# Residual tiles and output laid out by row block, then sequence, then channel; residual loads in eight transfers a tile

## The chip, the core and the metric

The kernel runs on one core of a Trainium2 chip. A core has a matrix engine (TensorE, PE in the profile), a vector engine (VectorE, DVE), an activation engine (ScalarE, ACT), a general engine (GpSimd, POOL), and a sequencer that mostly issues DMAs (SyncE, SP); sixteen DMA engines move data between HBM and the on-chip memory SBUF. The metric is device time in microseconds of one execution, the median of several.

## What is computed

x is [32 sequences, 64 channels, 1024 positions] in float32. Four layers follow one another, each added to its input:

```python
x = x + L0(x)   # long convolution per channel (state-space kernel), masked by length
x = x + L1(x)   # einsum('bsi,boi->bso', x, weight[adapter])   1024 x 1024, one of 16 per sequence
x = x + L2(x)   # the same with a second set of weights
x = x + L3(x)   # gate and up (1024 -> 2752), silu(gate) * up, down (2752 -> 1024), each with a rank-16 adapter
```

The last line is where the change lies. Its `x +` needs the input of the last layer again, the residual, once the down projection has produced its part.

## The kernel before

Positions lie on the 128 partitions: position = 128 * l + partition, with l = 0..7 (LT = 8) the row block. A tile is TB = 8 sequences of H = 64 channels, 512 columns; there are NTILE = 4 tiles, handled in NST = 2 stages of two tiles each (j = 0, 1). The last layer's matmuls are split by a Strassen-like scheme with seven products, and every product in three passes of rounded high and low parts (`three`, lines 2289 to 2291).

After the second layer the input of the third is stored in HBM as `kept_rows` (`xs`, [P, B, LT, H]: for each partition sequence, then block, then channel). The down projection of a stage (`down(st)` on TensorE) runs through eleven products: d1, d5, l11, d2, d6, l21, d4, d7, l12, d3, l22. A d product has five panels, an l product two; together NSIDE = 43 panels, counted by `panel_done`. For each panel n, ScalarE rounds the weights and the activations to `wdh` and `th` and VectorE forms the low parts `wdl` and `tl` (helper line 1642), while SyncE loads the raw panels three ahead at most. The buffers of the cut panels are doubled.

Between these cuts, in an order written out by hand (`take_product(st, n)`), VectorE adds each finished product from the matmul banks, or from a carry (`tmp`), into the residual tiles `resid[0]` and `resid[1]` (helper line 1645). These additions are called takes here. A product in the banks has the shape [P, 4 blocks, 512 columns], columns being sequence times channel, while `resid` is [P, TB, LT, H] (sequence, block, channel): the take reads the banks with strides. Tile 0 is first needed at panel n = 9, tile 1 at n = 11, just between the cut of the side and the cut of the row that the first panel of d2 (n = 12) needs.

GpSimd issues the residual loads (`load_residual`, line 789): tile 0 once four panels have ended, tile 1 after seven. In stage 0 it then issues sixteen loads of the next stage's rows (`load_rows`, line 797, to `rraw`), four each after panels 9, 11, 13 and 16; these already read `kept_rows` one block at a time. Afterwards it stores the halves of the residual tiles as they become complete (`store`, line 783), and SyncE stores the last half tile in three parts (line 713). The waits on `resid_in` count 16 for each transfer. GpSimd does all this in order.

Of the kernel before, what the change touches and what calls it, by code (L numbers as in the profile page):

```python
# [16 lines left out]
F32 = mybir.dt.float32  # L17
# [5 lines left out]
P = 128  # L23
B, H, L = 32, 64, 1024
LT = L // P
# [29 lines left out]
NTILE = ROWS // TILE  # L55
TB = TILE // H
# [69 lines left out]
def sides(st, n):  # L126
    return st * NSIDE + n
# [31 lines left out]
def build(nc, ins, out):  # L159
    with ExitStack() as ctx:  # L160
        sem = lambda name: ctx.enter_context(nc.semaphore(name))

        def sb(stack, name, shape, dt=F32):
            return stack.enter_context(nc.sbuf_tensor(name, shape, dt))
# [3 lines left out]
        xs = nc.dram_tensor("kept_rows", [P, B, LT, H], F32).ap()  # L168
# [82 lines left out]
        def placed(offset, above="main"):  # L251

            s = ExitStack()
            if offset:
                sb(s, f"below_{above}", [P, offset // 4])
            return s
# [9 lines left out]
        with placed(OPS_AT) as s:  # L266
# [5 lines left out]
            rows = [sb(s, f"rows{k}", [P, KH, TILE], F32R) for k in range(14)]  # L272
# [1 line left out]
            tmp = sb(s, "tmp", [P, 6, TILE])  # L274
            lraw = sb(s, "lraw", [P, GR, 2, P])
        with placed(0) as s:
            resid = [sb(s, f"resid{j}", [P, TB, LT, H]) for j in range(2)]
        with placed(OPS_AT, "wdh") as s:
            wdh = sb(s, "wdh", [P, 2, LT * P], F32R)
            th0 = sb(s, "th0", [P, 2 * TILE], F32R)  # L280
# [18 lines left out]
        carry = tmp[:, 2:6]  # L299
# [21 lines left out]
        ps = ctx.enter_context(nc.psum_tensor("ps", [P, 8, 512], F32))  # L321
# [94 lines left out]
        taken = sem("taken")  # L416
        carried = sem("carried")
        resid_in = [sem(f"resid_in{j}") for j in range(2)]
        y_out = sem("y_out")
        last_out = sem("last_out")  # L420
# [9 lines left out]
        def _(sp):  # L430
# [279 lines left out]
            for k, (ready, o, width) in enumerate(((10, 0, 4), (12, 4, 2), (14, 6, 2))):  # L710
                mine = slice(o, o + width)
                sp.wait_ge(taken, end + ready)
                sp.dma_start(out[NTILE - 1, :, :, mine], resid[1][:, :, mine]).then_inc(last_out, 16)
            sp.wait_ge(last_out, 48)

# [1 line left out]
        def _(pool):  # L718
# [22 lines left out]
            for k in range(2):  # L741
                pool.iota(spare[:, k].rearrange("l (t u) -> l t u", u=2), pattern=[[0, STEPS // 2], [k, 2]],
                          base=B + 2 * (1 - k), channel_multiplier=0,
# [39 lines left out]
            def store(st, ready, j, half):  # L783

                pool.wait_ge(taken, st * NTAKE + ready)
                mine = slice(4 * half, 4 * half + 4)
                pool.dma_start(out[2 * st + j, :, :, mine], resid[j][:, :, mine]).then_inc(y_out, 16)

            def load_residual(tile):

                pool.wait_ge(x_saved[tile // 2], 16)
                for part in range(4):
                    mine = slice(2 * part, 2 * part + 2)
                    b0 = tile * TB + 2 * part
                    pool.dma_start(resid[tile % 2][:, mine], xs[:, b0:b0 + 2]).then_inc(resid_in[tile % 2], 16)

            def load_rows(st, part):

# [6 lines left out]
            def down_loads(st):  # L805

                for ended, tile, part in ((4, 0, None), (7, 1, None), (9, None, 0), (11, None, 1), (13, None, 2), (16, None, 3)):
                    if part is not None and st:
                        continue
                    pool.wait_ge(panel_done, sides(st, ended))  # L810
                    if part is None:
                        load_residual(2 * st + tile)
                    else:
                        load_rows(st + 1, part)
# [32 lines left out]
            for s in range(SEQ):  # L847
                gather_inner(1, s)
                gather_outer(1, s)
            down_loads(0)  # L850
            store(0, 5, 0, 0)
            store(0, 8, 0, 1)
            store(0, 10, 1, 0)
            store(0, 14, 1, 1)
            pool.wait_ge(y_out, 64)
# [442 lines left out]
        def _(dve):  # L1298
# [315 lines left out]
            base = 0  # L1614
            for layer in range(2):
# [11 lines left out]
                base = base + count  # L1627
# [16 lines left out]
            def add(to, a, b):  # L1644
                return V.tensor_tensor(out=to, in0=a, in1=b, op=ALU.add)  # L1645
# [311 lines left out]
            def take(st, p, half, j, blocks=range(4)):  # L1957

                o0, n = blocks[0], len(blocks)
                base = BANKS[p] + o0  # L1960
                rows = resid[j][:, :, 4 * half + o0:4 * half + o0 + n]
                add(rows, ps[:, base:base + n].rearrange("p o (b h) -> p b o h", h=H), rows).then_inc(taken, 1)

            def add_carry(st, p, ready):

                dve.wait_ge(carried, 3 * st + ready)
                add(carry, ps[:, BANKS[p]:BANKS[p] + 4], carry).then_inc(carried, 1)

            def take_carry(st, ready, half, j):

                dve.wait_ge(carried, 3 * st + ready)
                rows = resid[j][:, :, 4 * half:4 * half + 4]
                add(rows, carry.rearrange("p o (b h) -> p b o h", h=H), rows).then_inc(taken, 1)

            def take_product(st, n):

                if n == 9:
                    dve.wait_ge(resid_in[0], (st + 1) * 64)
                    take_carry(st, 1, 0, 0)
                if n in (11, 12):  # L1980
                    dve.wait_ge(resid_in[1], (st + 1) * 64)
                    dve.wait_ge(panel_done, sides(st, SIDE_AT["l11"]))
                    take(st, "d5", 0, 1, range(2 * (n - 11), 2 * (n - 10)))
                if n == 13:
                    take(st, "d5", 1, 1)
                if n == 21:
                    dve.wait_ge(panel_done, sides(st, SIDE_AT["d6"]))
                    dve.wait_ge(taken, st * NTAKE + 1)
                    take(st, "d2", 0, 0)
                if n == 25:  # L1990
                    dve.wait_ge(panel_done, sides(st, SIDE_AT["l21"]))
                    add_carry(st, "d6", 1)
                if n == 33:
                    dve.wait_ge(panel_done, sides(st, SIDE_AT["d7"]))
                    take(st, "d4", 1, 0)
                if n == 34:
                    dve.wait_ge(taken, st * NTAKE + 3)
                    take_carry(st, 2, 0, 1)
                if n == 37:
                    dve.wait_ge(panel_done, sides(st, SIDE_AT["l12"]))  # L2000
                    dve.wait_ge(taken, st * NTAKE + 7)
                    add_carry(st, "d7", 2)
                if n == 38:
                    dve.wait_ge(taken, st * NTAKE + 6)
                    take_carry(st, 3, 1, 0)
                if n == 39:
                    dve.wait_ge(taken, st * NTAKE + 4)
                    take_carry(st, 3, 1, 1)
                if n == NSIDE - 1:
                    dve.wait_ge(panel_done, sides(st, SIDE_AT["l22"]))  # L2010
                    dve.wait_ge(taken, st * NTAKE + 7)
                    take(st, "d3", 0, 1)
# [105 lines left out]
            for st in range(NST):  # L2118
# [21 lines left out]
                for n in range(2, NSIDE):  # L2140
                    whole = n < NSIDE - 1 and n + 1 not in AFTER_SHORT
                    if whole:
                        add_side(st, n + 1)
                    panel_lo(st, n)
                    if whole:
                        add_row(st, n + 1)
                    if n + 2 in AFTER_SHORT:
                        add_side(st, n + 2)
                        add_row(st, n + 2)
                    if n == 3:  # L2150
                        down_ranks(st)
                    take_product(st, n)
                    if st == 0:
                        new_rows_lo(n)
# [440 lines left out]
```

## Time and profile before

| | |
|---|---|
| Median of 3 runs | 2087.67 us (2087.14 to 2090.92) |
| The profiled execution | 2089.7 us |
| Its span, first to last instruction | 2088.0 us |
| Granted TensorE clock, mean | 0.998 of full speed |
| TensorE matmul busy | 2025.6 us, 97% |
| VectorE busy | 1756.0 us, 84% |
| ScalarE busy | 989.9 us, 47% |
| GpSimd busy | 134.8 us, 6% |

All times in rows are microseconds from the start of the span, unless a row says ns. PE is TensorE's matmuls, PEld its weight loads. `L1642` is line 1642 of the kernel. A group of instructions is named by what it writes and reads (out<-in). "busy" is the time in which the engine executes. A wait is put down to what ended it; "issue" means that nothing the profile shows ended it.

### The profile page before, as it was taken

Reading aid. Unit: us, or ns where it says so; the run is one execution under the profiler, and the core shown is the slowest. Engines: PE = TensorE matmul, PEld = TensorE weight load, DVE = VectorE, ACT = ScalarE, POOL = GpSimd, SP = SyncE. Lnnn points to the kernel's source line nnn. Section 1 sums busy time; section 2 is a strip of 40 time slices with the busy share of each in tenths; the row PEclk is TensorE's granted clock in tenths of the full one; section 3 lists DMA queues with packets and bytes.
Section 4 is the critical chain, followed back from the end, with each engine's and each line's share of the span. In section 5 each row is a group of like instructions: output and inputs, shape, how many; then the busy total and the mean of one; then the engine's idle time right before and its main releaser. Section 6 shows DMA issues by size and latency. Waiting matters only on the chain.

```text
span 2088.0 us, 33689 instructions
## 1 busy us (share of the span) xinstructions
PE 2025.6 (97%) x10192; PEld 1722.8 (83%) x10192; DVE 1756.0 (84%) x2203; ACT 989.9 (47%) x1255; POOL 134.8 (6%) x229
## 2 busy tenths in 40 slices
PE   2999999999999999999999999999999999999998
PEld 1998888878888788888888888888888888888887
DVE  8796999999999988878787779979788787868787
ACT  2221888878886534343343443454343333434332
POOL 3100000000000323210000020010000000000000
PEclk9999999999999999999999999999999999999999
DMA  6997999999999556754334996645334333368665
GB/s 247 336 335 281 340 358 350 355 346 352 347 363 351 165 164 194 201 145 106 97 100 107 343 316 213 203 144 132 91 101 113 94 103 102 100 220 305 197 204 183
DMA packets 246432, 459.51 MB, mean 220 GB/s; under 512 B 110502, under 2 KB 113766, under 8 KB 226662
## 3 DMA queue, kind: packets, MB, share of 16 engines
q1 hardware_dynamic: 229250, 416.03, 59.6%
q0 software_dynamic: 14944, 42.50, 6.7%
q8 instruction: 30, 0.49, 0.1%
q10 hardware_dynamic: 2180, 0.26, 0.1%
q14 instruction: 28, 0.23, 0.0%
HBM read 418.56 MB, written 63.73 MB: 231 GB/s over the span
## 4 chain that ended last, share of the span: by engine, by line
PE 83%; DVE 9%; DMA 3%; issue 2%; ACT 2%; DVEq 0%; ACTq 0%; SPq 0%
PE ps L2289 19%; PE ps L2290 19%; PE ps L2291 19%; PE ps L2183 5%; PE ps L2211 5%; PE ps L2213 5%; PE ps L2212 5%; DMA W<-in_w 2%; PE ps L2367 2%; PE ps L2368 2%; DVE part L1550 1%; PE ps L2220 1%; PE ps L2404 1%; PE ps L2405 1%; DVE rows L1642 1%
## 5 line engine op out<-in xcount | busy, mean ns | idle before, releaser
L2289 PE MATMUL ps<-rows,oph 128*128 128x512 f32 x1196 | 467.2, 391 | 1.1 <-DVE opl L1642 0.6
L2290 PE MATMUL ps<-rows,oph 128*128 128x512 f32 x1196 | 466.9, 390 | 0.0
L2291 PE MATMUL ps<-rows,opl 128*128 128x512 f32 x1196 | 465.3, 389 | 0.0
L1550 DVE TENSOR_TENSOR part<-W,part 128x2048 fp32r<-128x2048 f32 x152 | 344.1, 2289 | 14.0 <-ACT part L902 13.2
L1645 DVE TENSOR_TENSOR tmp<-ps,tmp 128x512 f32<-128x512 f32 (+2 forms) x344 | 242.9, 707 | 106.0 <-PE ps L2368 61.0
L902 ACT ACTIVATE part<-W 128x2048 fp32r<-128x2048 f32 x152 | 290.9, 1917 | 84.5 <-DMA W<-in_w 58.5
L2291 PEld LDWEIGHTS ps<-rows,opl 128*128 128x128 f32 x1196 | 224.6, 188 | 47.7
L2289 PEld LDWEIGHTS ps<-rows,oph 128*128 128x128 f32 x1196 | 225.0, 188 | 45.5 <-DVE opl L1642 1.9
L2290 PEld LDWEIGHTS ps<-rows,oph 128*128 128x128 f32 x1196 | 225.0, 188 | 41.8
L2289 PE MATMUL ps<-th,wdh 128*128 128x512 f32 (+1 forms) x656 | 249.4, 380 | 1.6 <-DVE tl L1642 1.1
L2290 PE MATMUL ps<-tl,wdh 128*128 128x512 f32 (+1 forms) x656 | 248.6, 379 | 0.0
L2291 PE MATMUL ps<-th,wdl 128*128 128x512 f32 (+1 forms) x656 | 248.5, 379 | 0.0
L967 ACT ACTIVATE oph<-sraw 128x512 fp32r<-128x512 f32 x168 | 105.9, 631 | 284.9 <-PE ps L2291 255.6
L2211 PE MATMUL ps<-part,rh 128*128 128x512 f32 x600 | 237.3, 395 | 0.5 <-issue 0.3
L2213 PE MATMUL ps<-part,rl 128*128 128x512 f32 x600 | 233.8, 390 | 0.0
L2212 PE MATMUL ps<-part,rh 128*128 128x512 f32 x600 | 233.7, 389 | 0.0
L2183 PE MATMUL ps<-urev,toep 128*128 128x256 f32 (+7 forms) x1024 | 151.5, 311 | 9.2 <-issue 9.1
L2183 PEld LDWEIGHTS ps<-urev,toep 128*128 128x128 f32 x1024 | 147.0, 194 | 13.5 <-issue 9.6
L967 ACT ACTIVATE wdh<-wraw 128x1024 fp32r<-128x1024 f32 (+1 forms) x66 | 66.6, 1009 | 172.1 <-PE ps L2291 167.1
L2289 PEld LDWEIGHTS ps<-th,wdh 128*128 128x128 f32 x656 | 123.4, 188 | 27.4 <-issue 2.5
L2291 PEld LDWEIGHTS ps<-th,wdl 128*128 128x128 f32 x656 | 123.4, 188 | 23.3
L2290 PEld LDWEIGHTS ps<-tl,wdh 128*128 128x128 f32 x656 | 123.4, 188 | 22.7
(246 smaller groups left out, 3027.1 us busy)
## 6 DMA issues: line engine op xcount, KB each, us to landing
W<-in_w SPq DMA_DIRECT2D x152, 1024.0 KB, 7.1
raw<-in_wgu SPq DMA_DIRECT2D x168, 256.0 KB, 2.8
traw<-kept_acts SPq DMA_DIRECT2D x78, 512.0 KB, 4.9
wraw<-in_wd SPq DMA_DIRECT2D x70, 512.0 KB
toep<-kpad SPq DMA_DIRECT2D x32, 1024.0 KB, 8.8
lraw<-picked_b SPq DMA_DIRECT2D x88, 256.0 KB, 4.0
kept_acts<-tmp SPq DMA_DIRECT2D x84, 256.0 KB, 2.4
urev<-in_urev SPq DMA_DIRECT2D x32, 256.0 KB, 6.7
```

The source lines that it names most:

```text
L902: nc.scalar.activation(wh[c][:], W[:, c], ACT.Copy).then_inc(w_hi, 1)
L967: return nc.scalar.activation(to, src, ACT.Copy)
L1550: V.tensor_tensor(out=wl[c][:], in0=W[:, c], in1=wh[c][:].bitcast(F32), op=ALU.subtract).then_inc(w_lo, 1)
L1645: return V.tensor_tensor(out=to, in0=a, in1=b, op=ALU.add)
L2183: last = mm(ps[:, i % RING, (e + 1) * LT * B - n:(e + 1) * LT * B], lhsT=toep[:, i % RING, e, d * P:(d + 1) * P], rhs=rows[:, 0:n], start= ...
L2211: mm(bank(o), lhsT=rh[:, at], rhs=wh[c][:, k], start=first, stop=False)
L2212: mm(bank(o), lhsT=rh[:, at], rhs=wl[c][:, k], start=False, stop=False)
L2213: last = mm(bank(o), lhsT=rl[:, at], rhs=wh[c][:, k], start=False, stop=end)
L2289: mm(to, lhsT=wh, rhs=mh, start=start, stop=False)
L2290: mm(to, lhsT=wh, rhs=ml, start=False, stop=False)
L2291: return mm(to, lhsT=wl, rhs=mh, start=False, stop=stop)
L2367: mm(ps[:, to, cols], lhsT=lt[:, g, c], rhs=tmh[:, c, g], start=start and g % 2 == 0, stop=False)
```

## The change

`resid` and the output `y` get the order block, sequence, channel. A take then reads and writes one run of columns for each block, as the banks have them. The residual load is cut into eight transfers, one for each block, since `kept_rows` keeps its order (sequence, block, channel): a transfer reads, for each partition, eight pieces of 64 floats. The semaphore values follow, and the host puts the output in order with another transpose.

```diff
@@ -274,7 +274,7 @@
         with placed(0) as s:
-            resid = [sb(s, f"resid{j}", [P, TB, LT, H]) for j in range(2)]
+            resid = [sb(s, f"resid{j}", [P, LT, TB, H]) for j in range(2)]
@@ -710,7 +710,7 @@
                 mine = slice(o, o + width)
                 sp.wait_ge(taken, end + ready)
-                sp.dma_start(out[NTILE - 1, :, :, mine], resid[1][:, :, mine]).then_inc(last_out, 16)
+                sp.dma_start(out[NTILE - 1, :, mine], resid[1][:, mine]).then_inc(last_out, 16)
@@ -784,15 +784,14 @@
                 mine = slice(4 * half, 4 * half + 4)
-                pool.dma_start(out[2 * st + j, :, :, mine], resid[j][:, :, mine]).then_inc(y_out, 16)
+                pool.dma_start(out[2 * st + j, :, mine], resid[j][:, mine]).then_inc(y_out, 16)
 
             def load_residual(tile):
 
                 pool.wait_ge(x_saved[tile // 2], 16)
-                for part in range(4):
-                    mine = slice(2 * part, 2 * part + 2)
-                    b0 = tile * TB + 2 * part
-                    pool.dma_start(resid[tile % 2][:, mine], xs[:, b0:b0 + 2]).then_inc(resid_in[tile % 2], 16)
+                for l in range(LT):
+                    pool.dma_start(resid[tile % 2][:, l], xs[:, tile * TB:(tile + 1) * TB, l]
+                                   ).then_inc(resid_in[tile % 2], 16)
@@ -1958,8 +1957,8 @@
-                rows = resid[j][:, :, 4 * half + o0:4 * half + o0 + n]
-                add(rows, ps[:, base:base + n].rearrange("p o (b h) -> p b o h", h=H), rows).then_inc(taken, 1)
+                rows = resid[j][:, 4 * half + o0:4 * half + o0 + n].rearrange("p o b h -> p o (b h)")
+                add(rows, ps[:, base:base + n], rows).then_inc(taken, 1)
@@ -1969,16 +1968,16 @@
-                rows = resid[j][:, :, 4 * half:4 * half + 4]
-                add(rows, carry.rearrange("p o (b h) -> p b o h", h=H), rows).then_inc(taken, 1)
+                rows = resid[j][:, 4 * half:4 * half + 4].rearrange("p o b h -> p o (b h)")
+                add(rows, carry, rows).then_inc(taken, 1)
 
             def take_product(st, n):
 
                 if n == 9:
-                    dve.wait_ge(resid_in[0], (st + 1) * 64)
+                    dve.wait_ge(resid_in[0], (st + 1) * LT * 16)
                     take_carry(st, 1, 0, 0)
                 if n in (11, 12):
-                    dve.wait_ge(resid_in[1], (st + 1) * 64)
+                    dve.wait_ge(resid_in[1], (st + 1) * LT * 16)
@@ -2587,8 +2586,8 @@
-    out = nc.dram_tensor("y", [NTILE, P, TB, LT, H], F32, kind="ExternalOutput").ap()
+    out = nc.dram_tensor("y", [NTILE, P, LT, TB, H], F32, kind="ExternalOutput").ap()
-    return np.ascontiguousarray(y.transpose(0, 2, 4, 3, 1).reshape(B, H, L))
+    return np.ascontiguousarray(y.transpose(0, 3, 4, 2, 1).reshape(B, H, L))
```

## Rows read from the trace of the kernel before

**Rows 1.** The page's busy line, and TensorE's waits in 1150 to 1400 us.

```profile
PE 2025.6 (97%) x10192; PEld 1722.8 (83%) x10192; DVE 1756.0 (84%) x2203; ACT 989.9 (47%) x1255; POOL 134.8 (6%) x229
...
PE ps L2289 <- DVE tl L1642: 1.1, 2, 0.7
```

**Rows 2.** VectorE by form, 1150 to 1400 us: busy us, mean ns, idle before.

```profile
L1645 DVE TENSOR_TENSOR resid<-tmp,resid 128x2048 f32<-128x2048 f32 x4 | 9.1, 2286 | 0.0
L1645 DVE TENSOR_TENSOR resid<-ps,resid 128x2048 f32<-128x2048 f32 x4 | 9.1, 2285 | 0.0
...
L1645 DVE TENSOR_TENSOR tmp<-ps,tmp 128x2048 f32<-128x2048 f32 x2 | 4.6, 2287 | 0.0
```

**Rows 3.** GpSimd's timeline, stage 0: start, duration, engine, line, count, [idle before].

```profile
1179.50 2.13 POOL L795 DMA_DIRECT2D resid<-kept_rows  x4 [271.45 <-PE ps L2291]
1196.65 2.08 POOL L795 DMA_DIRECT2D resid<-kept_rows  x4 [15.02 <-issue]
1206.70 3.55 POOL L802 DMA_DIRECT2D rraw<-kept_rows  x4 [7.97 <-PE ps L2291]
1215.01 2.64 POOL L802 DMA_DIRECT2D rraw<-kept_rows  x3 [4.77 <-PE ps L2291]
1225.75 4.37 POOL L802 DMA_DIRECT2D rraw<-kept_rows  x5 [8.11 <-issue]
```

**Rows 4.** Instructions on `kept_rows`: ns min/median/max, first and last start.

```profile
L795 POOL DMA_DIRECT2D resid<-kept_rows x16: 527/536/564, 1179.5 to 1907.9; - x16
L802 POOL DMA_DIRECT2D rraw<-kept_rows x16: 882/882/915, 1206.7 to 1242.2; - x16
```

**Rows 5.** Single `rraw` loads in short windows: their start and their landing.

```profile
L802 POOL DMA_DIRECT2D rraw<-kept_rows x1: 915/915/915, 1206.7 to 1206.7; - x1
DMA to landing us min/median/max: 4.7/4.7/4.7
...
L802 POOL DMA_DIRECT2D rraw<-kept_rows x1: 884/884/884, 1216.8 to 1216.8; - x1
DMA to landing us min/median/max: 8.5/8.5/8.5
...
L802 POOL DMA_DIRECT2D rraw<-kept_rows x2: 882/882/882, 1228.4 to 1229.2; - x2
DMA to landing us min/median/max: 8.8/9.8/10.7
```

**Rows 6.** GpSimd's DMA queue, packets, MB, share; 1178 to 1196, 1206 to 1250.

```profile
q0 software_dynamic: 576, 2.10, 32.1%
...
q0 software_dynamic: 1280, 4.20, 38.1%
```

**Rows 7.** Timeline of VectorE and TensorE around the first takes, stage 0.

```profile
1204.42 2.29 DVE L1645 TENSOR_TENSOR resid<-tmp,resid 128x2048 f32<-128x2048 f32 x1
...
1213.32 1.23 DVE L1645 TENSOR_TENSOR resid<-ps,resid 128x1024 f32<-128x1024 f32 x1
...
1215.90 1.23 DVE L1642 TENSOR_TENSOR wdl<-wraw,wdh 128x1024 fp32r<-128x1024 f32 x1 [0.23 <-ACT wdh L967]
...
1217.30 0.39 PE L2289 MATMUL ps<-th,wdh 128*128 128x512 f32 x1
```

**Rows 8.** The same in stage 1: tile 1 loaded and first used.

```profile
1906.33 2.10 POOL L795 DMA_DIRECT2D resid<-kept_rows  x4 [14.15 <-PE ps L2291]
...
1923.83 1.23 DVE L1645 TENSOR_TENSOR resid<-ps,resid 128x1024 f32<-128x1024 f32 x1
```

**Rows 9.** VectorE's timeline: the reader of the first eight `rraw` loads.

```profile
1232.69 2.29 DVE L1642 TENSOR_TENSOR rraw<-rraw 128x2048 f32<-128x2048 f32 x1 [0.78 <-DMA rraw<-kept_rows]
```

**Rows 10.** The end: SyncE's stores and wait; its DMA queue, 2079 to 2088 us.

```profile
2079.13 3.47 SPq L713 DMA_DIRECT2D y<-resid  x3
...
SPq L160 <- DMA y<-resid: 5.0, 1, 5.0
...
q1 hardware_dynamic: 3120, 2.10, 76.4%
```

## Prediction

> **What bounds the kernel now.** I read the page's busy shares first: the matmul engine is busy 97% of the span [rows 1]. So a saving on any other engine is worth nothing unless the matmul engine waits for it, and a new delay counts as soon as the work queued for it runs out. The change touches only the two down-projection stages (roughly 1180 to 1375 us and 1890 to 2088 us). The list of waits for the first of them shows the matmul engine waiting for VectorE twice, 1.1 us in all [rows 1]. The stages are therefore bound by TensorE, with VectorE close behind. In them VectorE cuts the operands of each panel of weights and does the "takes" (adding a product to a residual tile) between the cuts. The questions are: do the takes get shorter, do the residual tiles still come in time, and what does the end cost?
>
> **Takes.** All 28 change from blocks of 64 floats with strides to one run. In the trace a take of 128x2048 with the old strides is 2286 or 2285 ns, and the same size without any stride (`tmp<-ps,tmp`, the carry) is 2287 ns [rows 2]. Strides of this kind cost nothing here, so the takes stay as they are: 0 us, bounds within 0.1.
>
> **Residual loads, issue.** Before, a tile is four transfers of 0.53 us on GpSimd (4 KB in one piece per partition). After, it is eight, each made of 1024 pieces of 256 B. That is exactly the form of the 16 loads of `rraw` from `kept_rows` in line 802, which take 0.88 us each to issue [rows 4]. A tile's issue grows from 2.1 to 7.0 us.
>
> **Residual loads, transfer.** Four loads of a tile used 32.1% of 16 engines in 18 us, or 92 engine-us for 2.10 MB: 44 per MB. The 16 `rraw` loads used 38.1% in 44 us, or 268 for 4.20 MB: 64 per MB [rows 6]. A tile becomes 134 engine-us, 2.6 us more of all 16 engines. The Trainium skill, "DMA: Bandwidth & Descriptors", section on why small descriptors are slow, gives 11 cycles where 8 move data for a 256 B descriptor; as an estimate that makes 127 engine-us instead of 134. The rows show somewhat more than the page, and I go by the rows.
>
> **Residual loads, a wait in the queue.** In the timeline of GpSimd, loads of this form start at 1206.70 (four) and 1215.01 (three); the eighth, which waits for no semaphore of the program, starts only at 1225.75, after 8.11 us that the trace puts down to "issue" [rows 3]. The seventh was issued 1.76 us after 1215.01 and landed 8.5 us later, at 1225.27 [rows 5]: 0.48 us before the eighth started. I read this as room for seven such transfers in the queue of descriptors, and a wait for the seventh to land (they share a semaphore) before the eighth is written. The Trainium skill, same page, section "SWDGE vs HWDGE vs iDMA", says that GpSimd appends these descriptors to rings in a reserved part of SBUF. It states no such wait; only the row shows one. A tile after the change is eight such transfers in a row on one semaphore, so I expect the eighth of every tile to wait likewise: four waits, two in each stage.
>
> **When does a tile land?** From its first issue: the first load lands after 4.7 us [rows 5] to 6.9 us (issued at 1225.75, its reader starts at 1232.69) [rows 3, 9]. The next ones follow at the pace of the engines. Lower bound 134/8/16 = 1.05 us each, if nothing else moves; upper bound 1.8 us, the pace of five in a row beside SyncE's panel loads (the first lands by 1232.69, the fifth at 1229.2 + 10.7 = 1239.9, four steps) [rows 5, 9]. I take 1.6, nearer to the upper one, since SyncE's loads are in flight here too. The seventh lands at 4.7 + 6 x 1.6 = 14.3 us (bounds 11.0 and 17.7); the eighth is issued 0.5 later and lands in 5.5 us (4.7 to 6.9). The tile is there after 20.3 us (16.2 to 25.1), where now it takes some 10 us.
>
> **Tile 0** starts at 1179.50 and is first used at 1204.42 [rows 3, 7], 24.9 us later: covered, but for the upper bound by 0.2 us. **Tile 1** starts at 1196.65 and is used at 1213.32 [rows 3, 7], 16.7 us later. It lands at 1216.95, 3.6 us late. Behind that take VectorE has queued the row cut and the cut `wdl` at 1215.90 (which waited 0.23 for ScalarE and ends at 1217.13), and TensorE starts on that panel at 1217.30 [rows 7]. The slack is 0.23 + 0.17 = 0.4 us, so TensorE loses 3.2 us (bounds 0 and 8.0). In the second stage tile 1 starts at 1906.33 and is used at 1923.83 [rows 8], 17.5 us: 2.8 us late, 2.4 lost with the same slack (0 to 7.2). TensorE has no idle time later in which to make this good.
>
> **What stands behind tile 1 on GpSimd.** The `rraw` loads due at 1206.70 [rows 3] start at about 1212.4. Their consumer on VectorE at 1232.69 already waits 0.78 us for them [rows 9], but it will itself be 3.2 us late by then. I take 0.3 us (0 to 3). The slower transfers also squeeze SyncE's panel loads; the cover is the 1.2 to 2 us by which VectorE's cuts lead TensorE. Nothing in the trace prices this beyond the 1.1 us of rows 1; I take 0.3 us (0 to 2).
>
> **Stores.** Their runs in HBM grow from 1 KB (512 B for the last two) to 8 KB (4 KB). Nobody waits for the six that GpSimd issues while TensorE works on; I cost them at nothing, and their cover is the matmuls of the following panels (a single one of them costs a few tenths of a us if it were bare). The last three are bare: SyncE issues them from 2079.13 on and then waits 5.0 us for them. They use 76.4% of 16 engines in 9 us for 2.10 MB, 52 engine-us per MB, in 3120 packets [rows 10]. At the 44 per MB of 4 KB packets [rows 6] that is 8 x 2.1 / 16 = 1.1 us less, and the last issue gets a little shorter: -1.2 us (-2 to 0).
>
> **Sum.** 3.2 + 2.4 + 0.3 + 0.3 - 1.2 = +5.0 us. The profiled execution took 2089.7 us, of which 2088.0 are the span and 1.7 lie around it; it would become 2094.7. The median of the runs is 2.0 us below the profiled one, so I predict 2087.7 + 5.0 = 2092.7 us.
>
> **Rivals.**
> The tile comes in time (not slower). If the eighth load doesn't wait, it lands at 4.7 + 7 x 1.6 = 15.9 us, before the 16.7 of tile 1. The 8.11 us would then be something particular to that moment; it is a single event, which speaks for this rival, and its end on the landing of the seventh speaks against it. The same comes out if it waits but the transfers keep near the 1.05 us pace. Then 0.5 us of side costs and -1.2 remain: 2087.0 us. The turning point is a tile in 17 us. Chance 0.35.
> Pile-up (clearly slower). The transfers run at 1.8 us or worse, tile 0's eighth load goes out after 1196.65 and pushes tile 1, and each stage loses near its upper bound: 7 + 6 + 1 - 1.2, about +13 us, 2100.5 us. Against it: SyncE's loads pause while VectorE stands still, which lets the others through. Chance 0.10.
> Cheaper takes (faster). If single runs made VectorE faster after all, the last take, which nothing covers, would shorten, and the late tile would be caught up partly. Against it stand the equal durations of rows 2. To be faster by over 4 us TensorE would have to have been waiting for VectorE, and rows 1 give 1.1 us. About 2084 us, chance 0.03.
> The stores don't change: if the packets at the end stay small, the sum only loses its -1.2: 2093.9 us, inside the forecast's own range.
>
> **How the numbers follow.** A measurement of this kernel tells about 0.2%, 4.2 us, from no change. The forecast, a late tile 1, has a chance of 0.52 and its own range is 2089.5 to 2098; a good quarter of it ends under 2091.9. So slower by over 0.2%: 0.38 + 0.10 = 0.48. Within 0.2%: 0.35 + 0.14, with the rounding 0.48. Faster: 0.04. The range reaches from just under the first rival to the top of the forecast, 2086.3 to 2098.0; it leaves out the pile-up, the cheaper takes and some of the edges.
>
> **What would show it.** In the timeline of GpSimd after the change: eight loads a tile of 0.88 us, seven and then a gap of 7 to 9 us, four times. In VectorE's waits: the first `resid<-ps` of 128x1024 in each stage waiting for `resid<-kept_rows`, some 3 us. In TensorE's waits: the same, less 0.4, at the first panel of `d2`. The takes at 2285 ns as before. Some 500 packets instead of 3072 in the last stores, and SyncE's last wait near 4 us. The prediction is wrong if the gap is missing, if the tile lands within 17 us of its start despite it, or if VectorE's cuts after the late take turn out to have more slack than 0.4 us.

## The result, and the profile after

The changed kernel took 2100.39 us (median of 4 runs, 2098.84 to 2103.28), the kernel before, on the same chip, 2087.40 us. The ratio is 1.0057 [1.0045, 1.0068]: slower by some 12 us by the ratio (13.0 us between the medians), above the forecast of 2092.7 us and above its range (2086.3 to 2098.0). It is the number that the rival "pile-up" gave, 2100.5 us, though not for its reasons alone, as shown further down. The profiled execution took 2099.75 us, and its span is 2098.1 us against 2088.0 us before: the rows have 10.1 us to explain; the rest is where the two profiled executions lie among their runs.

The page's busy line:

```profile
PE 2026.9 (97%) x10192; PEld 1724.0 (82%) x10192; DVE 1755.5 (84%) x2203; ACT 990.9 (47%) x1255; POOL 152.6 (7%) x245
```

Beside [rows 1] only GpSimd's line has moved, by 16 instructions and 18 us of issuing. VectorE does what it did. Nothing in the busy shares tells of 10 us, because the loss lies in a few waits of TensorE. These are its waits in 1150 to 1400 us (stage 0), then in 1870 to 2099 us (stage 1), each with total, number and longest in us:

```profile
PE ps L2288 <- DVE wdl L1641: 5.9, 1, 5.9
PE ps L2288 <- DVE tl L1641: 1.4, 2, 0.7
...
PE ps L2288 <- DVE tl L1641: 2.2, 1, 2.2
PE ps L2288 <- DVE wdl L1641: 1.8, 1, 1.8
```

Before there were 1.1 us in stage 0 [rows 1] and none of this kind in stage 1. To see who is late, go back one step: the timeline of VectorE (lines 1641 and 1644), of ScalarE (966) and of TensorE (2288) around these waits, first stage 0, then stage 1 (start, duration, what, and in brackets the idle time and what ended it):

```profile
1219.16 1.23 DVE L1644 TENSOR_TENSOR resid<-ps,resid 128x1024 f32<-128x1024 f32 x1 [7.42 <-DMA resid<-kept_rows]
1222.71 0.80 PE L2288 MATMUL ps<-th,wdh 128*128 128x512 f32 x1 [5.89 <-DVE wdl L1641]
...
1929.66 1.06 ACT L966 ACTIVATE th<-traw 128x1024 fp32r<-128x1024 f32 x1 [3.98 <-DMA traw<-kept_acts]
1930.75 1.23 DVE L1641 TENSOR_TENSOR tl<-traw,th 128x1024 fp32r<-128x1024 f32 x1 [3.82 <-ACT th L966]
1932.12 0.36 PE L2288 MATMUL ps<-th,wdh 128*128 128x256 f32 x1 [2.17 <-DVE tl L1641]
1936.19 1.23 DVE L1644 TENSOR_TENSOR resid<-ps,resid 128x1024 f32<-128x1024 f32 x1 [3.61 <-DMA resid<-kept_rows]
1939.74 0.50 PE L2288 MATMUL ps<-th,wdh 128*128 128x512 f32 x1 [1.76 <-DVE wdl L1641]
```

In stage 0 the first take into tile 1 starts at 1219.16 us instead of 1213.32 us [rows 7], and the panel of d2 behind it at 1222.71 instead of 1217.30. In stage 1 two things are late: first `traw`, a panel of activations that SyncE loads, and then tile 1 again.

GpSimd's timeline shows why tile 1 is late (stage 0, then stage 1):

```profile
1178.78 6.19 POOL L793 DMA_DIRECT2D resid<-kept_rows  x7 [270.23 <-issue]
1193.76 7.01 POOL L793 DMA_DIRECT2D resid<-kept_rows  x8 [8.79 <-issue]
1212.28 0.88 POOL L793 DMA_DIRECT2D resid<-kept_rows  x1 [11.51 <-issue]
...
1897.62 6.17 POOL L793 DMA_DIRECT2D resid<-kept_rows  x7 [505.24 <-PE ps L2290]
1913.28 6.13 POOL L793 DMA_DIRECT2D resid<-kept_rows  x7 [9.49 <-issue]
1919.89 0.88 POOL L793 DMA_DIRECT2D resid<-kept_rows  x1 [0.48 <-issue]
1930.97 0.88 POOL L793 DMA_DIRECT2D resid<-kept_rows  x1 [10.20 <-issue]
```

A tile is seven loads and then, after a gap, the eighth: the gaps are 8.79, 11.51, 9.49 and 10.20 us. The rows merge what follows without idle time: the one at 1193.76 with its eight loads is tile 0's eighth with the first seven of tile 1 right behind it, and the one at 1913.28 is tile 0's eighth with six of tile 1, whose seventh is the row at 1919.89 and whose eighth is the one at 1930.97. Before, GpSimd's queue had 15.02 us of rest between the tiles [rows 3]; now the tiles touch. The landings in stage 0 of tile 0's eighth load together with tile 1's first (5.7 us the former alone, so 6.0 us the latter), then of tile 1's seventh, then of its eighth:

```profile
L793 POOL DMA_DIRECT2D resid<-kept_rows x2: 882/883/884, 1193.8 to 1194.6; - x2
DMA to landing us min/median/max: 5.7/5.9/6.0
...
L793 POOL DMA_DIRECT2D resid<-kept_rows x1: 891/891/891, 1199.9 to 1199.9; - x1
DMA to landing us min/median/max: 12.0/12.0/12.0
...
L793 POOL DMA_DIRECT2D resid<-kept_rows x1: 882/882/882, 1212.3 to 1212.3; - x1
DMA to landing us min/median/max: 6.9/6.9/6.9
```

The seventh lands at 1211.9 us and the eighth goes out at 1212.28, as [rows 3, 5] had it with 0.48 us between the two. The tile is complete at 1219.16 us.

Then there is a loss that stands in no wait. The windows of 1222 to 1228 and 1236 to 1242 us: length, busy time of PE, PEld, DVE, ACT, POOL with counts, then the granted clock, the share of the DMA engines and GB/s:

```profile
1222.00:1228.00 6.00, 5.29 (x13) 4.14 (x13) 6.00 (x5) 0.00 (x0) 0.00 (x0) 0.50 1.03 250
1236.00:1242.00 6.00, 6.00 (x29) 4.95 (x28) 4.11 (x3) 2.01 (x2) 0.00 (x0) 1.00 1.01 310
```

After its 5.9 us of idling TensorE was granted 0.50 of its clock, that is 1.2 GHz, until about 1228.7 us. Thirteen matmuls of 512 columns followed each other at 0.43 us where they do at 0.23 us from 1236 us on: 2.7 us.

Last the end: SyncE's stores, its wait for them, and the packets of its queue in the last 9 us. They answer to [rows 10]:

```profile
2091.18 3.03 SPq L713 DMA_DIRECT2D y<-resid  x3
...
SPq L160 <- DMA y<-resid: 3.4, 1, 3.4
...
q1 hardware_dynamic: 432, 2.10, 56.8%
```

432 packets instead of 3120, 56.8% of the engines instead of 76.4%, and 0.4 + 1.6 = 2.0 us gained.

The account: stage 0 lost 5.9 + 0.3 us in waits and 2.7 at half the clock, stage 1 lost 2.2 + 1.8 us, the end gave back 2.0 us: 10.9 us. The kernel came to the first of the two stages 0.7 us earlier (1178.78 against 1179.50). That leaves 10.2 us, against 10.1 in the spans. So close a match is partly luck: GpSimd's first load of stage 1 goes out at 1897.62 instead of 1890.02 us, 7.6 us later, where the account up to there has 8.2, and stage 1 has half a us more than its waits.

### The profile page after: what moved, and what is told of

Read it like the earlier page. It is cut to its first block, busy times and chain, and to the rows that moved or that the text cites. A ratio compares the mean times of both kernels' runs of the same rounds, so it can differ in the third digit from the quotient of the medians.

```text
span 2098.1 us, 33705 instructions
## 1 busy us (share of the span) xinstructions
PE 2026.9 (97%) x10192; PEld 1724.0 (82%) x10192; DVE 1755.5 (84%) x2203; ACT 990.9 (47%) x1255; POOL 152.6 (7%) x245
## 4 chain that ended last, share of the span: by engine, by line
PE 80%; DVE 9%; issue 4%; DMA 4%; ACT 2%; POOL 1%; DVEq 0%; ACTq 0%; SPq 0%; POOLq 0%
PE ps L2288 18%; PE ps L2289 18%; PE ps L2290 18%; PE ps L2182 5%; PE ps L2210 5%; PE ps L2212 5%; PE ps L2211 5%; DMA W<-in_w 3%; PE ps L2366 2%; PE ps L2367 2%; POOL resid L793 1%; PE ps L2219 1%; DVE part L1549 1%; PE ps L2403 1%; PE ps L2404 1%
## 5 line engine op out<-in xcount | busy, mean ns | idle before, releaser
L1549 DVE TENSOR_TENSOR part<-W,part 128x2048 fp32r<-128x2048 f32 x152 | 343.2, 2286 | 10.9 <-ACT part L901 10.2
```

Of the source, the lines that this page charges most:

```text
L1549: V.tensor_tensor(out=wl[c][:], in0=W[:, c], in1=wh[c][:].bitcast(F32), op=ALU.subtract).then_inc(w_lo, 1)
```

## The experiments

In the diffs only the lines that carry the experiment are shown; semaphore values and the like that follow from them are left out.

Theory at this point: the eight loads of 256 B pieces cost the whole loss, through the wait of the eighth and the slow landing behind it; takes and stores cost nothing or gain. The rivals are that the number of transfers does it, or the new order of the tile (takes, stores), or crowding of the DMA engines with or without the wait.

### One part at a time

The changed kernel with the four loads of before, 4 KB in one piece for each partition:

```diff
-                for l in range(LT):
-                    pool.dma_start(resid[tile % 2][:, l], xs[:, tile * TB:(tile + 1) * TB, l]
-                                   ).then_inc(resid_in[tile % 2], 16)
+                for part in range(4):
+                    mine = slice(2 * part, 2 * part + 2)
+                    b0 = tile * TB + 2 * part
+                    pool.dma_start(resid[tile % 2][:, mine].rearrange("p l b h -> p l (b h)"),
+                                   xs[:, b0:b0 + 2].rearrange("p b l h -> p b (l h)")).then_inc(resid_in[tile % 2], 16)
```

> The changed kernel with the residual loads of the kernel before: four transfers a tile, 4 KB in one piece per partition. The values land in the wrong order (block, sequence and channel are mixed up), so the output is not the reference's; bytes, takes and stores are those of the changed kernel. My theory (all of the loss is in the eight-part loads, and takes and stores only gain at the end): 2085.4 us, 2 below the kernel before, takes of 2285 ns, PE waits of about 1 us in the first down stage. Rival (the new layout of takes or stores costs something itself): above 2088 us.

Measured: 2086.69 us against 2089.48, ratio 0.9987 [0.9976, 0.9999]. TensorE waits 1.5 us in stage 0 in two waits (1.1 us before), and SyncE's last wait is 3.5 us. So takes and stores in the new order lose nothing and gain about 2.8 us (0.2 to 5 us by the interval), and all the loss sits in the loads.

The other half, the kernel before with only the eight loads, into the old layout:

```diff
-                for part in range(4):
-                    mine = slice(2 * part, 2 * part + 2)
-                    b0 = tile * TB + 2 * part
-                    pool.dma_start(resid[tile % 2][:, mine], xs[:, b0:b0 + 2]).then_inc(resid_in[tile % 2], 16)
+                for l in range(LT):
+                    pool.dma_start(resid[tile % 2][:, :, l], xs[:, tile * TB:(tile + 1) * TB, l]
+                                   ).then_inc(resid_in[tile % 2], 16)
```

> The kernel before with only its residual loads cut into eight, one for each block, into the old order in SBUF (256 B pieces on both sides); takes and stores as before. My theory: the loss of the changed kernel plus the 2 us that its end gains, about 2102 us, with the same gaps of 8 to 11 us before the eighth load of a tile. Rival (the loss comes from an interplay with the new layout): near 2088 us.

Measured: 2102.95 us, ratio 1.0069 [1.0050, 1.0089], 14 us slower. The gaps are there (9.24 and 10.60 us in stage 0), and TensorE's waits in stage 0 and stage 1 come near those of the changed kernel, though in stage 1 nearly all of it is now one wait for `tl`:

```profile
PE ps L2288 <- DVE wdl L1641: 4.7, 1, 4.7
PE ps L2288 <- DVE tl L1641: 1.9, 2, 1.3
...
PE ps L2288 <- DVE tl L1641: 3.9, 2, 3.6
```

The two halves add up: 14 - 3 = 11 us, near the 12 of the whole change.

### Number of transfers, or size of their pieces

Eight loads a tile, each with 2 KB in one piece for a partition:

```diff
-                    pool.dma_start(resid[tile % 2][:, l], xs[:, tile * TB:(tile + 1) * TB, l]
-                                   ).then_inc(resid_in[tile % 2], 16)
+                    pool.dma_start(resid[tile % 2][:, l].rearrange("p b h -> p (b h)"),
+                                   xs[:, tile * TB + l].rearrange("p l h -> p (l h)")).then_inc(resid_in[tile % 2], 16)
```

> The changed kernel with eight residual loads a tile of the same bytes, but each in one piece of 2 KB per partition on both sides (block l is filled with the rows of sequence l, so values land in the wrong places and the output is not the reference's). If the 256 B pieces are the cause: no gap before the eighth load, issues near 0.5 us, time as with the old loads, 2085 to 2087 us. Rival (eight transfers instead of four cost by their number): above 2090 us.

Measured: 2087.83 us against 2088.85, ratio 0.9998 [0.9988, 1.0007]. The eight loads of tile 1 go out without a gap, at 0.53 us each:

```profile
1194.82 4.24 POOL L793 DMA_DIRECT2D resid<-kept_rows  x8 [11.64 <-PE ps L2290]
```

It is not the number of transfers. It is the 1024 pieces of 256 B that each of them is made of in the changed kernel.

### The wait of the eighth

One semaphore for each of the eight loads, instead of one that counts them all:

```diff
-        resid_in = [sem(f"resid_in{j}") for j in range(2)]
+        resid_in = [[sem(f"resid_in{j}_{l}") for l in range(LT)] for j in range(2)]
@@
-                                   ).then_inc(resid_in[tile % 2], 16)
+                                   ).then_inc(resid_in[tile % 2][l], 16)
@@
-                    dve.wait_ge(resid_in[0], (st + 1) * LT * 16)
+                    for l in range(LT):
+                        dve.wait_ge(resid_in[0][l], (st + 1) * 16)
```

> The changed kernel with a semaphore of its own for each of the eight loads of a tile; VectorE waits for all eight. If the eighth load waits because the room in the queue can only be taken back when the shared semaphore has reached its newest count: now only the first load has to have landed, the gap falls from 8.8 to under 2 us, and the time to about 2090 us. If room is only given back when the whole queue is empty, or the loss is only the pace of the small pieces: gaps and time stay, 2100 us.

Measured: 2101.2 us, ratio 1.0054 [1.0037, 1.0070]. The time is as bad as with the gaps, but the long gaps are gone, and other work is late. The profiled execution is the longest of the six (2107.3 us) and came to stage 0 5.4 us later than the kernel before, so its waits, not its length, are to be read here. GpSimd's timeline, and the rows of ScalarE and TensorE behind it, in stage 0:

```profile
1184.91 7.11 POOL L793 DMA_DIRECT2D resid<-kept_rows  x8 [275.89 <-issue]
1200.51 6.15 POOL L793 DMA_DIRECT2D resid<-kept_rows  x7 [8.49 <-PE ps L2292]
1208.19 0.88 POOL L793 DMA_DIRECT2D resid<-kept_rows  x1 [1.54 <-issue]
...
1220.18 1.06 ACT L966 ACTIVATE th<-traw 128x1024 fp32r<-128x1024 f32 x1 [7.36 <-DMA traw<-kept_acts]
1222.64 0.55 PE L2290 MATMUL ps<-th,wdh 128*128 128x256 f32 x1 [5.54 <-DVE tl L1641]
```

Tile 0 goes out eight in a row, and tile 1's eighth waits 1.54 us instead of 11.51 (2.84 us in stage 1). Tile 1's first load goes out at 1200.51 us and lands 7.4 us later, at 1207.9, and the eighth starts 0.3 us behind that (in stage 1 it is 1927.7 and 1928.02): now it is the first load that has to have landed, as the expectation had it. VectorE no longer waits for `resid` at all. Yet TensorE idles 5.5 us, now for `tl`, because `traw` has not landed. SyncE's panel loads issued between 1196 and 1216 us, in this kernel (count, KB each, median us to landing):

```profile
traw<-kept_acts SPq DMA_DIRECT2D x3, 512.0 KB, 15.0
```

(15.0 us too in the window moved by 5.4 us), then in the kernel before and in the changed kernel:

```profile
traw<-kept_acts SPq DMA_DIRECT2D x4, 512.0 KB, 9.1
...
traw<-kept_acts SPq DMA_DIRECT2D x4, 512.0 KB, 11.6
```

So the reading of the wait was right in that the count on the shared semaphore holds the eighth back. My expectation that the time would come back with it was wrong. With the wait tile 1 is late and SyncE's panels are somewhat later; without it tile 1 is in time and the panels are later still. The Trainium skill, "DMA: Bandwidth & Descriptors", section "Queues, rings and completion order", says that a DMA engine goes in turn through the queues that have work, a packet at a time. The trace agrees in so far as SyncE's panels land after 15.0 us instead of 9.1 when the small pieces go out without the gap; no run here shows the turns themselves.

Room for more descriptors, 8704 bytes instead of 8192:

```diff
-    nc = bacc.Bacc("TRN2", target_bir_lowering=False, num_devices=1, dynamic_dma_scratch_size=8192)
+    nc = bacc.Bacc("TRN2", target_bir_lowering=False, num_devices=1, dynamic_dma_scratch_size=8704)
```

 My theory (room for seven but not eight): no gap, eight issues in 7.1 us, tile 1 there about 18 us after its first issue instead of 24.6, time 2088 to 2091 us. Rival (the pace of the pieces beside the panel loads is all): landing and time stay at 2098 to 2101 us, whatever the gap does.

Measured: 2095.63 us, ratio 1.0028 [1.0016, 1.0040]. Now eight fit, in the tile and in the `rraw` loads behind it:

```profile
1195.78 7.02 POOL L793 DMA_DIRECT2D resid<-kept_rows  x8 [9.93 <-issue]
1214.06 7.02 POOL L801 DMA_DIRECT2D rraw<-kept_rows  x8 [11.26 <-issue]
```

Tile 1's eighth load lands at 1213.6 us, 17.9 us after the tile's first went out at 1195.78; about 18 was expected. VectorE waits 1.4 us for tile 1 instead of 7.4, and TensorE in stage 0 for `wdl` and `tl`, in stage 1 for `tl`:

```profile
PE ps L2288 <- DVE tl L1641: 2.7, 3, 1.4
PE ps L2288 <- DVE wdl L1641: 1.6, 1, 1.6
...
PE ps L2288 <- DVE tl L1641: 4.6, 2, 3.8
```

The step from seven to eight with 6% more room shows that the limit is room for descriptors. Half of the loss against the kernel before is gone, not all, and the time is above the 2088 to 2091 us expected. Stage 1's longest wait is `traw` again, which lands after 12.5 us (issues between 1905 and 1930 us) instead of 4.4 before. So the wait can be taken away in two ways, and they did not come to the same: own semaphores gained nothing (1.0054), more room gained half (1.0028). No run shows why.

### Which tile

Tile 0 with the loads of before, tile 1 in pieces:

```diff
+                if tile % 2 == 0:
+                    for part in range(4):
+                        mine = slice(2 * part, 2 * part + 2)
+                        b0 = tile * TB + 2 * part
+                        pool.dma_start(resid[0][:, mine].rearrange("p l b h -> p l (b h)"),
+                                       xs[:, b0:b0 + 2].rearrange("p b l h -> p b (l h)")).then_inc(resid_in[0], 16)
+                    return
```

> The changed kernel, but tile 0 of each stage is loaded as before the change (four transfers, 4 KB in one piece per partition, values misplaced, so the output is not the reference's); tile 1 keeps its eight loads of 256 B pieces. If the late tile 1 is made by its own queue wait and pace: it still lands more than 20 us after its first issue and TensorE still waits some 5 us, 2093 to 2096 us. If it is the backlog that tile 0 leaves on the engines and in SyncE's loads: tile 1 lands within 20 us, time below 2091 us.

Measured: 2097.4 us, ratio 1.0039 [1.0024, 1.0054]. GpSimd's timeline for tile 1 in stage 0, and the waits of VectorE and TensorE:

```profile
1195.35 6.18 POOL L800 DMA_DIRECT2D resid<-kept_rows  x7 [15.00 <-issue]
1210.29 0.88 POOL L800 DMA_DIRECT2D resid<-kept_rows  x1 [8.76 <-issue]
...
DVE resid L1651 <- DMA resid<-kept_rows: 4.4, 1, 4.4
PE ps L2295 <- DVE wdl L1648: 3.8, 1, 3.8
```

With nothing small of tile 0 ahead of it, VectorE waits 4.4 us for tile 1, not 7.4, and TensorE's longest wait is 3.8 us; in stage 1 it is 3.4 us. The eighth load lands 6.1 us after 1210.29 us, so the tile takes 21.1 us from its first load (at 1195.35) to its last landing, against 24.5 us in the changed kernel: the 3.4 us between them are what tile 0's small pieces cost tile 1. By itself tile 1 comes near the forecast's 20.3 us, and its 4.4 us of lateness near the forecast's 3.6. More than 20 us to the landing is what was expected if its own wait and pace make it late, and most of the loss is here; the time is a little above the 2093 to 2096 us expected.

### Keeping the order and paying elsewhere

If small pieces are the cost, the loads can stay small only where they have time, or the rows can be put in order earlier. The first: small pieces in two halves a tile, each half with its own semaphore. Tile 1's go out after panels 6 and 7, the second half of tile 0 only after panel 18:

```diff
-                for ended, tile, part in ((4, 0, None), (7, 1, None), (9, None, 0), (11, None, 1), (13, None, 2), (16, None, 3)):
+                for ended, tile, part in ((4, 0, None), (6, 2, None), (7, 3, None), (9, None, 0), (11, None, 1), (13, None, 2), (16, None, 3),
+                                          (18, 1, None)):
```

> The changed kernel with its small pieces, but only the blocks that are needed soon are loaded in the busy stretch: blocks 0 to 3 of tile 0 after panel 4, blocks 0 to 3 of tile 1 after panel 6, blocks 4 to 7 of tile 1 after panel 7 (needed two panels later), blocks 4 to 7 of tile 0 after panel 18 (needed at panel 33); each half on its own semaphore. Bytes and pieces in all are the same. If crowding in the busy stretch is the cause: the late tile disappears and what is left is 1 to 4 us of waiting for panel loads, 2087 to 2090 us. If the pieces cost by their total, wherever they are: no better than 2096 us.

Measured: 2090.4 us against 2088.85, ratio 1.0008 [0.9998, 1.0017]. The longest wait of TensorE is 2.9 us in stage 0 and 1.0 in stage 1, both for `tl`:

```profile
PE ps L2291 <- DVE tl L1642: 3.6, 2, 2.9
```

Most of the loss is gone, though the pieces are no fewer and no larger: 1.7 us are left against the kernel before, some 4 against the changed kernel with the old loads. So it is not the total of small pieces that costs. The run does not separate its parts: it moves a quarter of the pieces out of the crowded stretch, starts tile 1 a panel earlier, gives each half its own semaphore, and lets VectorE wait for tile 1's second half two panels later.

The second, `kept_rows` stored by block when it is written, by SyncE:

```diff
-        xs = nc.dram_tensor("kept_rows", [P, B, LT, H], F32).ap()
+        xs = nc.dram_tensor("kept_rows", [P, NTILE, LT, TB, H], F32).ap()
@@
-                    part = slice(k * SEQ, (k + 1) * SEQ)
-                    sp.dma_start(xs[:, part], X[:, part]).then_inc(x_saved[k], 16)
+                    for t in (2 * k, 2 * k + 1):
+                        for l in range(LT):
+                            sp.dma_start(xs[:, t, l], X[:, t * TB:(t + 1) * TB, l]).then_inc(x_saved[k], 16)
```

> The changed kernel with the rows kept in HBM by tile, block, sequence, channel: they are stored in 32 transfers of 256 KB by SyncE, with runs of 256 B on the SBUF side, and both residual loads (four a tile again) and the loads of the next rows then read one run of 2 or 4 KB per partition. Correct values. My theory: both down stages as with the old loads or better, 2085 us, if the 32 stores around 660 us stay hidden. Rival (the stores hold up what waits for the rows to be saved, or SyncE's next loads behind them): the wait moves to the stretch from 660 to 700 us, 5 to 20 us, 2090 to 2105 us.

Measured: 2102.8 us, ratio 1.0071 [1.0059, 1.0083]. The down stages are clean, and the price has moved to 657 us: SyncE's timeline there, and the waits of ScalarE and TensorE that follow:

```profile
657.31 39.22 SPq L537 DMA_DIRECT2D kept_rows<-X  x32
...
ACT oph L966 <- DMA kept_rows<-X: 18.0, 1, 18.0
...
PE ps L2366 <- DVE tml L1641: 16.7, 1, 16.7
```

SyncE needs 39 us to issue the 32 stores, 1.2 us each, and ScalarE may not overwrite X until they have landed: TensorE stands still for 16.7 us. This is the rival of the expectation, and it came true. What stands behind a moved step decides here too.

The third, GpSimd copies `kept_rows` inside HBM into block order between 903 and 953 us, when nothing waits for GpSimd, and the tiles are loaded from there in long runs:

```diff
+        xb = nc.dram_tensor("kept_blocks", [P, NTILE, LT, TB, H], F32).ap()
@@
+                pool.wait_ge(relaid, 16 * NTILE * LT)
+                for part in range(4):
+                    mine = slice(2 * part, 2 * part + 2)
+                    pool.dma_start(resid[tile % 2][:, mine], xb[:, tile, mine]).then_inc(resid_in[tile % 2], 16)
@@
+            pool.wait_ge(x_saved[1], 16)
+            for t in range(NTILE):
+                for l in range(LT):
+                    pool.dma_start(xb[:, t, l], xs[:, t * TB:(t + 1) * TB, l]).then_inc(relaid, 16)
```

> The changed kernel; rows are kept in HBM as before, and GpSimd, once the gathers of the adapters are through (about 908 us, its queue is then idle until 1178), copies them inside HBM into block order, 32 copies of 256 KB in 256 B pieces, one after the other. The residual tiles and the next rows are loaded from that copy in runs of 2 to 4 KB. Correct values. Expected by my theory (small pieces only cost where the engines are crowded; between 900 and 1150 us they are 36 to 50% busy): both down stages as with the old loads, 2085 to 2086 us, 0.999. Rival (the copies starve SyncE's weight loads in the unit loop): TensorE waits there, 2090 us or more.

Measured: 2085.67 us against 2088.24, ratio 0.9984 [0.9975, 0.9994]. This version is faster than the changed kernel and, by 2.6 us, a little faster than the kernel before; that is what the run with the old loads gained, the short end. GpSimd's timeline: the first row of the copy, which goes out in sevens with gaps once more, then a tile of stage 0:

```profile
903.30 6.13 POOL L854 DMA_DIRECT2D kept_blocks<-kept_rows  x7 [4.91 <-issue]
...
1193.30 2.10 POOL L797 DMA_DIRECT2D resid<-kept_blocks  x4 [14.13 <-PE ps L2296]
```

TensorE is busy without a break from 900 to 960 us, and in the down stages its longest wait is 0.7 us. The 32 copies keep their small pieces and their gaps of 4 to 8 us, and cost nothing, because nobody is waiting there, although the DMA engines are 85% busy from 900 to 950 us instead of 50%.

The same copy in groups of three, spread over eleven steps (`units`) of the loop that runs in that stretch:

```diff
+                    k = t * LT + l
+                    if k % 3 == 0:
+                        pool.wait_ge(unit_step, at_step(0, 9 + k // 3, 0))
```

> As the relaid kernel, but three copies at a time, one group at the start of each of the units 9 to 19 instead of all in a row. If a row of 32 copies starves the weight loads: this one is faster than the unpaced one, 2085 us. If neither waits: both the same within 1 us.

Measured: 2085.68 us, ratio 0.9985 [0.9975, 0.9996]. Pacing brings nothing more.

## Why the prediction fell short, step by step

The forecast was +5.0 us. With each term as it was measured (the paragraphs below have them), it is 5.0 + 2.7 (tile 1 in stage 0) + 2.7 (the clock) + 2.2 (panel loads) - 0.6 (tile 1 in stage 1) - 0.3 (next rows) - 0.8 (the end) - 0.7 (the earlier start of stage 0, which nothing here explains) = 10.2 us, against 10.1 in the spans. The steps that failed are the landing time of tile 1, the price of SyncE's panel loads, and the clock, which the sum took as full throughout.

**The wait of the eighth load: right.** Four gaps, 8.8 to 11.5 us; a little longer than the 7 to 9 that I expected, because the seventh lands later. It had been read off a single event [rows 3, 5].

**Issue, takes, tile 0: right.** 0.88 us a load; takes at 2284 and 2285 ns as in [rows 2]; VectorE did not wait for tile 0.

**When tile 1 lands: the term that was mis-sized.** The first load went out at 1194.64 us, the seventh landed 17.3 us later (forecast 14.3, upper bound 17.7), the eighth took 6.9 us (forecast 5.5, upper bound 6.9). Together 24.5 us instead of 20.3, just under the upper bound of 25.1. The first load landed after 6.0 us instead of 4.7, and the pace behind it was (17.3 - 6.0) / 6 = 1.9 us a load instead of 1.6, just over my bound of 1.8. Two things failed. I took the pace under the bound of [rows 5, 9], a stretch in which no tile load ran; the run with tile 1 alone in pieces has 1.8 us a load ((14.5 - 3.9) / 6) and 21.1 us in all, so this is worth 0.8 us. And I assumed an empty queue in front, while tile 0's eighth went out only 0.88 us before tile 1's first; the same run puts 3.4 us on tile 0's small pieces. Against these 4.2 us stand 1.3 us that I had not foreseen either: tile 1's first load went out 15.9 us after tile 0's instead of 17.2. So the first take was 3.6 + 4.2 - 1.3 = 6.5 us late, and TensorE waited 5.9 us in stage 0 instead of 3.2.

**The rival "pile-up": near in number, partly by luck.** It had the slow pace and tile 0 pushing tile 1, at a chance of 0.10. But its condition that tile 0's eighth goes out after 1196.65 us did not come about (1193.76), and where it had the stages lose 7 and 6 us, tile 1 cost 5.9 and 1.8 us. The slow clock (2.7 us) and `traw` (2.2 us), which it did not name, filled the rest.

**Slack: right.** Against the old use, and counted from the start of the stage, the take came 5.8 + 0.7 = 6.5 us late and TensorE's panel behind it (1222.71 instead of 1217.30) 6.1 us: 0.4 us of cover, as I had it.

**Next rows: nothing lost.** Their loads went out at 1213.15 us, right behind tile 1, and VectorE did not wait for them: 0 instead of 0.3 us.

**Stage 1: total too small, and only partly for the cause given.** 2.4 us were forecast for tile 1; it cost 1.8, and here `traw` had already stopped TensorE for 2.2 us ahead of it. The tile itself took 22.0 us from its first load (1914.16) to its landing (1936.2).

**Squeeze on SyncE's panel loads: mis-sized.** I took 0.3 us for lack of a row, with 2 as the upper bound; it was 0.3 + 2.2 = 2.5 us. In stage 1 `traw` landed after 10.4 us (issues between 1905 and 1930 us) where it took 4.4 before. The runs with own semaphores and with 8704 bytes show that this term and the lateness of tile 1 hang together: take the wait away, and tile 1 gets earlier and the panels later (15.0 us in stage 0 with own semaphores; 12.6 and 12.5 us in stage 1). I should have asked what SyncE's loads lose to 45% more engine time per byte, not only what tile 1 loses.

**The clock: missing from the sum.** The wait of 5.9 us of TensorE went with some 6.8 us at 1.2 GHz, the last 0.9 us of the wait among them, worth 2.7 us. Shorter waits had it too: that of 3.4 us with tile 1 alone in pieces (stage 1), and that of 2.9 us in the run with halves, while the waits of 2.2 and 1.8 us in the changed kernel's stage 1 did not (1.00 throughout). Windows behind the first two, in that order:

```profile
1938.00:1941.00 3.00, 3.00 (x9) 2.32 (x8) 3.00 (x2) 0.00 (x0) 0.00 (x0) 0.50 0.99 373
...
1243.00:1245.00 2.00, 2.00 (x5) 1.61 (x6) 2.00 (x3) 1.06 (x1) 0.77 (x1) 0.50 0.99 312
```

So the wait of 3.2 us forecast for stage 0 was itself longer than one that was followed by the slow clock, and the sum should have had a term for it.

**Stores: right in mechanism, small in size.** -2.0 us in the profile instead of -1.2, within the bounds; -2.8 us in the run with the old loads.

What is open: what exactly is looked at before GpSimd's queue takes more transfers. That it is room (8704 bytes take eight, 8192 seven) and that the newest count of a shared semaphore stands for "all landed" (with own semaphores the eighth starts once the first has landed) is inferred from these runs. Open too is why the larger room gained half of the loss and own semaphores nothing, and why stage 0 and the first load of its tile 1 came early. Of the 15.0 us landing I can't tell how much is waiting for turns and how much is the engines' own time on small pieces.

## What to carry to other kernels

A load that is cut into 256 B pieces costs more than its own lateness: price it as engine time taken from every other queue in that stretch, and look at who has least cover there. A wait in a DMA queue that goes away need not be a gain while the engines are full: here it gained nothing one way and half of the loss the other way. Moving the small pieces to a stretch where nobody waits (a copy inside HBM, 250 us earlier) kept the short final stores and left the kernel 2.6 us faster than before the change. And a stall of the matmul engine of several us is to be priced with the slow clock behind it.

## What the runs showed of the hardware

- GpSimd's queue with 8192 bytes for descriptors took seven transfers of 1024 pieces at once, with 8704 bytes eight. The next one waited 8.8 to 11.5 us when all shared a semaphore, and 1.5 and 2.8 us when each had its own.
- A transfer of 256 KB took 0.88 us to issue on GpSimd in 256 B pieces and 0.53 us in 2 KB pieces; on SyncE, as a store of 256 B pieces, 1.2 us.
- Around a wait of 5.9 us without matmuls the granted clock was 0.50 for 6.8 us, most of them while TensorE was busy again (5.29 of 6 us). It fell to 0.50 with waits of 2.9 to 5.5 us in five other runs too, and not with waits of 2.2 us and less. With tile 1 alone in pieces, stage 0, it fell only 1.3 us after matmuls had resumed behind a wait of 3.8 us.
- Final stores in runs of 4 to 8 KB used 56.8% of 9 us for 2.10 MB, 39 engine-us per MB, against 52 in runs of 512 B to 1 KB [rows 10].
